# Rotary embedding on VectorE straight out of PSUM, and weight differences kept in DRAM: one change to a four-layer cross-attention kernel

## The reference

```python
vm = expert_mask(token_type_ids)[..., None]
mixed = jnp.where(vm, x @ v_qkv, x @ l_qkv)          # two experts, one per token
q, k, v = jnp.split(mixed, 3, axis=-1)
q, k = apply_rotary(q, k, position_ids, l)           # q * cos + rotate_half(q) * sin
ctx = sdpa(q, k, v, causal=True)
...
v_out = jax.nn.silu(mi @ v_gate) * (mi @ v_up) @ v_down
l_out = jax.nn.silu(mi @ l_gate) * (mi @ l_up) @ l_down
hidden_states = hidden_states + jnp.where(vm, v_out, l_out)
```

## Time and profile before

| | |
|---|---|
| Median of 3 runs | 2689.42 us (2686.3 to 2690.03) |
| The profiled execution | 2684.68 us, span of its instructions 2682.8 us |
| PE busy | 2560.8 us (95%), of it 109.3 us in pauses |
| DVE, ACT, POOL busy | 1534.7 us (57%), 1222.7 us (46%), 1155.9 us (43%) |
| Granted PE clock | 0.993 of full speed, mean over the span |
| DMA | 109.61 MB, 41 GB/s on average |

### The profile page before, as it was taken

One profiled execution on the slowest core, in us unless ns is written; L12 is line 12 of the kernel. 1 busy time (PEld: TensorE's weight loads), 2 busy tenths in 40 slices (PEclk: granted clock), 3 DMA queues, 4 the chain that ended last, 5 costly groups with the idle time before them and its releaser, 6 DMA issues.

```text
span 2682.8 us, 54240 instructions
## 1 busy us (share of the span) xinstructions
PE 2560.8 (95%) x20342; PEld 1554.7 (58%) x20342; DVE 1534.7 (57%) x3448; ACT 1222.7 (46%) x4274; POOL 1155.9 (43%) x1242
## 2 busy tenths in 40 slices
PE   6999999999999999999999999999999999999998
PEld 3556556665565656566555565665656556566565
DVE  2537556766434646776644464677644456467763
ACT  2335444644333635464433362654544346265462
POOL 0025265665211527656410342765641034267564
PEclk9999999999999999999999999999999999999999
DMA  8010011112201011121220101112121000120211
GB/s 211 1 32 2 22 44 48 41 41 72 72 2 32 2 41 40 32 58 31 70 68 1 32 2 52 38 28 60 29 72 60 9 25 2 52 60 10 55 41 44
DMA packets 171100, 109.61 MB, mean 41 GB/s; under 512 B 31764, under 2 KB 168408, under 8 KB 170712
## 3 DMA queue, kind: packets, MB, share of 16 engines
q1 hardware_dynamic: 166384, 105.82, 14.2%
q10 hardware_dynamic: 4456, 0.29, 0.2%
HBM read 101.87 MB, written 4.19 MB: 40 GB/s over the span
## 4 chain that ended last, share of the span: by engine, by line
PE 82%; DVE 11%; POOL 2%; issue 2%; ACT 1%; ACTq 1%; DMA 0%; SPq 0%; DVEq 0%
PE bank L1358 10%; PE bank L1375 6%; PE bank L1081 6%; PE bank L995 5%; PE bank L1244 4%; PE bank L1251 4%; PE bank L1263 4%; PE bank L1272 4%; PE bank L1364 3%; PE bank L1116 2%; PE bank L1298 2%; PE bank L1098 2%; PE bank L1057 2%; PE bank L1224 2%; PE bank L1070 2%
## 5 line engine op out<-in xcount | busy, mean ns | idle before, releaser
L1861 POOL TENSOR_TENSOR Ebuf<-Ebuf,row_rcp 128x512 f32<-128x512 f32 (+1 forms) x328 | 345.8, 1060 | 797.4 <-DVE row_rcp L1684 796.3
L1463 ACT ACTIVATE Ebuf<-bank,minus_max 128x64 f32<-128x64 f32 x1312 | 392.4, 334 | 39.8 <-DVE minus_max L1668 39.5
L1668 DVE TENSOR_REDUCE minus_max<-bank 128x8 f32<-128x512 f32 (+1 forms) x328 | 219.8, 673 | 161.2 <-PE bank L1070 81.2
L1463 ACT ACTIVATION_READ_ACCUMULATOR Ebuf<-bank,minus_max 128x1 f32 x1312 | 297.4, 227 | 0.0
L1472 ACT ACTIVATE PT<-bank 128x512 f32<-128x512 f32 (+1 forms) x328 | 192.6, 601 | 152.5 <-PE bank L1081 151.0
L1081 PE MATMUL bank<-ident,Ebuf 128*128 128x128 f32 x1296 | 201.5, 283 | 9.9 <-POOL Ebuf L1861 9.4
L1081 PEld LDWEIGHTS bank<-ident,Ebuf 128*128 128x128 f32 x1296 | 146.4, 143 | 64.5 <-issue 39.2
L1358 PE MATMUL bank<-xs_a,w_ring 128*128 128x512 f32 (+1 forms) x384 | 172.2, 611 | 7.7 <-POOL w_ring L1909 7.3
L1358 PE MATMUL bank<-xs_b,w_ring 128*128 128x512 f32 (+1 forms) x384 | 169.1, 602 | 5.9 <-POOL w_ring L1909 3.9
L1456 ACT ACTIVATE Ebuf<-Ebuf 128x512 f32<-128x512 f32 x160 | 102.0, 638 | 101.6 <-DVE Ebuf L1673 99.5
L1908 POOL TENSOR_TENSOR w_ring<-w_ring 128x256 f32<-128x256 f32 x192 | 131.9, 708 | 0.0
(11 more groups left out here) (325 smaller groups left out, 5599.6 us busy)
## 6 DMA issues: line engine op xcount, KB each, us to landing
w_ring<-in_L_W SPq DMA_DIRECT2D x64, 256.0 KB, 3.0
w_ring<-in_L_l_gate SPq DMA_DIRECT2D x80, 128.0 KB, 2.2
w_ring<-in_L_l_up SPq DMA_DIRECT2D x80, 128.0 KB, 2.3
w_ring<-in_L_l_down SPq DMA_DIRECT2D x80, 128.0 KB, 2.2
w_ring<-in_L_v_gate SPq DMA_DIRECT2D x80, 128.0 KB, 2.4
w_ring<-in_L_v_up SPq DMA_DIRECT2D x80, 128.0 KB, 2.4
w_ring<-in_L_v_down SPq DMA_DIRECT2D x80, 128.0 KB, 2.5
arena_a<-in_x SPq DMA_DIRECT2D x4, 512.0 KB
```

The costliest lines, as they stand in the source:

```text
L1463: last = A(Ebuf[:, u % UNITS, cell], bank(token)[:, cell], ACT.Exp, bias=minus_max[:, u % UNITS, c:c + 1], accum_out=row_sum[:, u % UNITS, ...
L1668: V.reduce_max(minus_max[:, u % UNITS, 0:g], cells(bank(token)[:, 0:g * S]), AX_X, negate=True).then_inc(maxed, 1)
L1861: G_.tensor_tensor(v, v, row_rcp[:, n % 3, 0:g].unsqueeze(2).broadcast_to([P, g, S]), ALU.mult).then_inc(probs_ready, 1)
```

## The change

Two things are edited, and both change the plan from which every engine's list is made.

**Rotary.** Steps `rot` and `rope` go; `qk` is now planned on PE and DVE. DVE multiplies the bank with the cosines, shuffles the same bank, multiplies with the sines and adds. ACT's copy and POOL's multiply go. The bank is free after the shuffle (`turned`).

**Differences.** Only group 0 (stream a, turn 0) runs `weigh`, and SP writes each difference to a DRAM tensor. All later chunks load expert l (three transfers) and the difference (one transfer, three for the last chunk); `g` waits for these transfers alone.

```diff
-    for i, (step, *where) in enumerate((("qk", 0), ("qk", 1), ("rot", 0), ("qk", 2), ("rot", 1), ("rope", 0), ("qk", 3),
-                                       ("rope", 1), ("rot", 2), ("v", 0), ("rot", 3), ("rope", 2), ("rope", 3), ("v", 1))):
+    for step, *where in (("qk", 0), ("qk", 1), ("qk", 2), ("qk", 3), ("v", 0), ("v", 1)):
...
+def first_use(token):
+
+    return token[1:3] == (0, 0)
...
-    return order
+    return [(when, token) for when, token in order if token[0] != "weigh" or first_use(token)]
...
-    if step == "rot":
-        return [("DVE", 1.45, None), ("POOL", 2.4, None)]
...
-BANK_FREE = {"g": 0.55, "sums": 0.25}
+BANK_FREE = {"g": 0.55, "qk": 1.45, "sums": 0.25}
...
+def begins_chunk(token):
+
+    return token[0] == "g" and not first_use(token) or token[0] == "l1h" and token[3] % 2 == 0
...
+    scratch = nc.dram_tensor("differences", (2 * FT, P, 3, DT * P), F32).ap()
...
-                for e in "lv":
+                if not first_use(key):
+                    q.wait_ge(*kept_at(layer, j))
+                    for dst, src in zip(rarer(rare_share(ring), j), rarer(scratch[FT * (layer - 2) + j], j)):
+                        q.dma_start(dst, src).then_inc(here, 16)
+                for e in "lv" if first_use(key) else "l":
...
+                elif step == "keep":
+                    n, j = where[2:]
+                    ring, _ = chunk("ffn", *where)
+                    q.wait_ge(weighed, FT * (n - 2) + j + 1)
+                    for dst, src in zip(rarer(scratch[FT * (n - 2) + j], j), rarer(rare_share(ring), j)):
+                        q.dma_start(dst, src).then_inc(kept_at(n, j)[0], 16)
...
-                            pe.wait_ge(*weighed[s].at(turn, FT * (n - 2) + j + 1))
+                            pe.wait_ge(*((weighed, FT * (n - 2) + j + 1) if first_use(token) else there))
...
-                if step == "qk":
-                    if where == [3, 0]:
-                        act.wait_ge(*hv_early[s].at(turn, FT))
-                    act.wait_ge(*filled(token))
-                    A(st.qk[:, where[1], :], bank(token)[:, :], ACT.Copy).then_inc(qk_ready[s].sem, 1)
...
-                if step == "rot":
+                if step == "qk":
...
+                    dve.wait_ge(*filled(token))
+                    V.tensor_tensor(by_batch(x), by_batch(bank(token)[:, :]), cos, ALU.mult).then_inc(cosined[s].sem, 1)
...
+                    V.stream_shuffle(v, bank(token)[:, :], PARTNER).then_inc(turned[s].sem, 1)
                     dve.wait_ge(*turned[s].at(turn, k + 1))
...
+                    V.tensor_tensor(by_batch(v), by_batch(v), sin, ALU.mult).then_inc(sined[s].sem, 1)
...
+                    V.tensor_tensor(x, x, v, ALU.add).then_inc(roped[s].sem, 1)
...
-                if step == "rot":
-                    n, i = where
-                    v = by_batch(st.qk[:, i, :])
-                    pool.wait_ge(*turned[s].at(turn, 4 * (n - 2) + i + 1))
-                    G_.tensor_tensor(v, v, cos_sin[:, 0, :].unsqueeze(1).broadcast_to([P, G, S]), ALU.mult).then_inc(cosined[s].sem, 1)
```

More of the change, by code:

```diff
@@ L324, in follows @@
             "zero_s": of("PE", ("wo", JT - 1)), "res2": of(None, ("w2", NF - 1)), "l1h": of(None, ("spread", 2, 0)) + of("PE", ("w2", (last or 0) - 3)),
[L325 to L326 removed]
+            "w2": of(None, ("l1h", last)), "res3": of(None, ("down", n, FT - 1)),
+            "cv": of(None, ("keys", n, 3)), "ck": of(None, ("keys", n, 3)) + of("PE", ("scores", ("self", n, 7))),
             "dense": of(None, ("pv", ("self", n, 4 * (last or 0) + 3))), "cq": of(None, ("spread", 4 if n == 2 else 7, last)),
@@ L396, in inputs @@
             for engine, t, name, *at in follows(step, turn, where):
+                if name == "weigh" and not first_use(token):
+                    continue
                 other = (name, s if name != "table" else 0, t, *at)
@@ L417, in room @@
             return slot()
-        if step == "l1h" and where[0] % 2 == 0:
+        if begins_chunk(token):
             there, free = slot(), banks(1)
@@ L503, in schedule @@
             heads[step, s].pop()
-            if step == "weigh":
-                chunks.append((("ffn", s, turn, *where), ("down", s, turn, *where)))
             if step == "l1h" and where[0] % 2 == 0:
                 chunks.append((("f1", s, turn, where[0] // 2), ("w2", s, turn, where[0] + 1)))
+            elif step == "weigh" or begins_chunk(token):
+                chunks.append((("ffn", s, turn, *where), ("down", s, turn, *where)))
             for j, (other, _, follow) in enumerate(pieces):
@@ L569, in transfers @@
         found.append((END[CHUNK_ENDS[n - SLOTS], "PE"] if n >= SLOTS else -1.0, ("chunk", *chunk)))
+    for token in ORDER["POOL"]:
+        if token[0] == "weigh":
+            found.append((END[token, "POOL"], ("keep", *token[1:])))
     return [token for _, token in sorted(found, key=lambda v: v[0])]
@@ L813, in emptied @@
         if step == "qk":
-            return qk_ready[s].at(turn, 4 * li + last + 1)
+            return turned[s].at(turn, 4 * li + last + 1)
         if step == "v":
@@ L836, in sums, with loads, kept_at, rarer @@
         return [banks[BANK["sum", m, accumulation(token)]] for m in range(DT)]
+    def loads(key):
+        return 2 if key[0] == "f1" else 6 if first_use(key) or key[4] == FT - 1 else 4
+    def kept_at(n, j):
+        m = CHUNKS["ffn", 0, 0, n, j]
+        before = [c for c, k in CHUNKS.items() if c[0] == "ffn" and first_use(c) and k <= m and k % SLOTS == m % SLOTS]
+        return kept[m % SLOTS], sum(16 * (3 if c[4] == FT - 1 else 1) for c in before)
+    def rarer(v, j):
+        if j < FT - 1:
+            return [v]
+        return [v[:, m, :].rearrange("p (k n) -> p k n", k=DT)[:, :, 0:FR] for m in range(2)] + [v[0:FR, 2, :]]
     def chunk(*key):
         n = CHUNKS[key]
-        count = sum(16 * (2 if c[0] == "f1" else 6) for c, m in CHUNKS.items() if m <= n and m % SLOTS == n % SLOTS)
+        count = sum(16 * loads(c) for c, m in CHUNKS.items() if m <= n and m % SLOTS == n % SLOTS)
         return w_ring[:, n % SLOTS, :], (chunk_loaded[n % SLOTS], count)
@@ L925, in load_chunk @@
                         q.wait_ge(*down_done[s].at(turn, FT * (where[0] - 2) + where[1] + 1))
+                    if step == "down" and first_use(CHUNK_ENDS[n - SLOTS]):
+                        q.wait_ge(*kept_at(*where))
                 here = chunk_loaded[n % SLOTS]
@@ L973, in _ @@
                 q.wait_ge(*stored[s].at(TURNS, 0))
+            for n in (2, 3):
+                for j in range(FT):
+                    q.wait_ge(*kept_at(n, j))
         @block.tensor
@@ L1343, in stages @@
                         rows = P if j < FT - 1 else FR
-                        ring, _ = chunk("ffn", s, turn, n, j)
+                        ring, there = chunk("ffn", s, turn, n, j)
                         w = ffn_weights(ring)[0][step]
```

33 lines of the change are left out of this document (16 added, 17 removed), and 2 rows, old and new, of the table own.

## The result

The changed kernel takes 2660.87 us (median) against 2689.73 us on the same chip, 28.9 us less: ratio 0.989, 95% interval 0.987 to 0.9909. One of its four executions was slow, 4284.32 us at a granted clock of 0.554, and is not in the ratio; the median of the other three is 2658.74 us, 31.0 us less than before. Timed again on another chip, the same kernel gave 2660.44 us and 0.9897 (0.9881 to 0.9914). The forecast was 2675 us: the sign was right and the time lies in the range, but the gain was more than double the 14.2 us of the sum.

The account below looks back on a forecast made before the run. PE was taken to bound the kernel, with only pauses and idle time able to change. Terms of -8.4, -11, +3.2 and +2 gave -14.2 us, from 2689.4 to 2675 us, range 2650 to 2695.

Parts of the forecast that it names:

- the sum: Total of the priced terms over the whole kernel: -8.4 - 11 + 3.2 + 2 = -14.2 us.
- What bounds it: PE bounds the kernel, busy 2560.8 of 2682.8 us; only 109.3 us of pauses and 122.0 us idle can change.
- the count of turns: Savings at `g` and the norm chain were counted for three of four turns, with turn 0 gaining nothing.
- 2451.5 us of PE's work, which the change leaves alone: PE's busy time without pauses, taken as unchanged by the edit.
- Norm chain, -11 (0 to -13): `spread`'s waits for DVE's norm links beside POOL's differences: three waits a turn, 1.2 us each, three turns.
- Wait of `g`, -8.4: PE's 11.2 us of waits at `g` for POOL's differences: three quarters go, -8.4 us.
- Transfers, 0: Loads of the kept differences before `g`, and turn 0's 16 writes, stay hidden: 0 us.
- Rotary, 0: Rotary block on DVE, 3.0 us against 2.79; PE waits only 0.2 us for keys, so 0 us.
- New plan, +3.2 and +2: Twelve more pauses on PE cost 3.2 us; pauses moved at stream a's norm 6 cost 2 us (0 to 6).
- The contention goes everywhere: Rival, chance 0.22: POOL's relief halves norm waits (23 us) and cuts waits for probabilities by a third; 2655 us.
- It gives nothing: Rival, chance 0.16: pauses run whether needed or not, so PE waits elsewhere and gives the gain back; 2687 us.
- DVE becomes late: Rival, chance 0.14: the unsplit rotary block delays norm links and maxima on DVE, 0.4 us per block; 2702 us.

Follow-up runs that it names:

- e6: The changed kernel itself, unaltered, timed once more on another chip: 2660.4 us, ratio 0.9897 to the kernel before.
- e1: Kernel before with only the differences made once and kept in DRAM; rotary, order and pauses as before: 2654.0 us, ratio 0.9872.
- e4: e1 with POOL doing subtractions of the same size and number in a spare buffer that nobody waits for: 2678.6 us, ratio 0.9965.
- e5: e4 with POOL's spare subtractions replaced by memsets, which write but read nothing: 2666.1 us, ratio 0.9914.
- e3: Kernel before with both edits, differences and rotary, but the old plan (order and 414 pauses): 2653.7 us, ratio 0.9874.
- e9: e3 with each step's pauses raised by a quarter, 529 for 414: 2652.3 us, ratio 0.9868.
- e10: e4 with the spare subtractions of each chunk done twice: 2771.4 us, ratio 1.0315.
- e2: Kernel before with only the rotary moved to DVE; differences and plan as before: 2681.4 us, ratio 0.9975.

## Why the prediction was right in sign and short in size

**What bounds it** stood in the main: idle time fell by 26.9 us where the sum had 17.4 (8.4 + 11 - 2). The mechanism was the one forecast, and two steps of the sum failed.

**The first step that failed is the count of turns.** "A quarter is turn 0's, where the differences are still made, so 3/4", and again "in the three turns that lose it: 3 x 3 x 1.2". `first_use` is `token[1:3] == (0, 0)`, stream a of turn 0 alone: 12 of that turn's 24 chunks. I had counted 84 of 96 gone for POOL's time and then went by 72 in both terms that matter. This is worth 6 us: 3.3 at the norm chain and 2.6 at `g`, the two waits of turn 0 that the changed kernel doesn't have. Turn 0 has the same stalled chain as the earlier trace rows, in the kernel before:

```profile
502.00 1.41 POOL L1908 TENSOR_TENSOR w_ring<-w_ring 128x256 f32<-128x256 f32 x2
...
502.77 0.65 DVE L1719 TENSOR_TENSOR norm_a<-norm_a 128x2 f32<-128x2 f32 x1
...
505.03 0.40 PE L1217 MATMUL bank<-ident,norm_a 128*128 128x128 f32 x2 [1.52 <-DVE norm_a L1731]
```

**The second is "2451.5 us of PE's work, which the change leaves alone"**, a term put at nothing. That work is not the same from one execution to the next. The changed kernel has 2454.9 us of it in one profiled execution, at a mean granted clock of 0.991, and 2448.3 in the other (e6), at 0.994, with idle times 1.8 us apart. The profiled execution of before had a clock of 0.993. Over its 37 executions beside the experiments those at 0.993 took 2684.7 us on average and those at 0.990 took 2689.9. My two profiled executions stand 9.3 us closer together than the medians, and the clocks fit: the one of before had a high clock for its kernel, the one of the changed kernel a low one (0.991, for 0.992 and 0.993 of its two others). Between before and e6, whose clocks are 0.993 and 0.994, the spans differ by 27.1 us: idle time -25.1, pauses +1.2, own work -3.2.

**Norm chain, -11 (0 to -13).** Setting the 104 `spread` steps of before and e1 side by side, 14 waits became shorter by more than 0.4 us, 16.6 us together: 3.3 in turn 0, 3.8 in each of turns 1 and 2, 5.7 in turn 3. The 3.6 us that I took for a turn was about right; turn 0 and two waits in turn 3, of 0.98 and 1.17 us, were missing. e4 and e5 show the mechanism, contention with POOL's subtractions and not with its memsets. The bound of 13 was too tight for e1; in the changed kernel the new plan gives back 3.6 us and 13.1 are left.

**Wait of `g`, -8.4.** Measured 9.4 in e1 and 11.2 in the changed kernel, where not even turn 0's is left.

**Transfers, 0.** Right: no wait for DMA at `g`, landing 3.5 us, and the 16 writes of turn 0 cost nothing that PE shows.

**Rotary, 0.** Right beside the differences (e3 against e1). By itself it is worth 6.3 us (4.0 to 9.4), and what the trace shows of it is 4.8 us less at `g`, by way of POOL's queue. The prediction didn't see that, since it set the rotary's price by PE's waits for the keys alone.

**New plan, +3.2 and +2.** The sum of 5.2 is near what was measured (4.5, from nothing to 9), but this is luck in part. The second part comes from turn 0 and not from norm 6: after the five pauses of stream a's norm 6 PE waits 0.06 us, not 0.3. The first part is not shown: e9 adds 24.1 us of pauses at no cost.

**The sum again** with these sizes: -11.2 (`g`) - 16.7 (norms) + 3.6 (norms, given back by the new plan) + 1.7 (pauses) - 2.6 (other waits) + 3.4 (own work) = -21.8 us, the difference of the profiled executions. The other 9.3 us are not in these two traces; they go with the clocks, as above. In e9, e1, e4 and e10 PE's own work goes with idle time (2440.1, 2448.5, 2451.3, 2482.7 us for 80.2, 94.8, 115.3, 177.7), as if idle time cost more than itself; that the change won some own work in this way is likely (the seven executions of the changed kernel that the ratios rest on have a mean clock of 0.992, the 37 of before 0.991), but not shown.

**The rivals.** "The contention goes everywhere" has nearly the right time (2655 to 2660 us) for partly wrong reasons: norm waits fell by 13 to 17 us and not 23, and the waits for probabilities didn't fall (9.4 to 10.2). "It gives nothing" and "DVE becomes late" are out: the pauses didn't eat the gain, and no wait for a bank that the shuffle frees, nor more than 0.4 us for L1716 (the old L1668), appears at PE.

## What to carry to other kernels

Price an auxiliary engine's work by what runs beside it: a short dependent chain on DVE, with PE waiting at its end, pays for POOL's subtractions and multiplies beside it, and removing these can be worth more than the wait for their result (here 15 to 17 us of waits against 9 to 11). Count how often an edit bites by its own condition in the code (stream and turn here), not by a round number of turns. Two edits that relieve one queue need not add up (33.7 and 6.3 us alone, 34.1 together); price each with the other in place. When two profiled executions are compared, compare their granted clocks too: 0.003 went with 5 us between executions of one kernel.

## What the runs showed of the hardware

- A DVE TENSOR_TENSOR or SCALAR_TENSOR_TENSOR of two columns took 0.16 us beside POOL's memsets (129 of 129 in e5), 0.57 to 0.65 us beside subtractions of 256 columns (0.71 to 0.78 us each), and 0.96 us beside multiplies of 512 (1.0 us each). The integer TENSOR_SCALAR of the chain took 1.17 us where a memset followed on a multiply beside it, and 0.78 us where a subtraction did.
- The rotary's instructions that read PSUM took 681 to 686 ns (multiply) and 726 to 728 ns (shuffle) in e2, in e3 and in the changed kernel, with POOL busy for 32% to 39% of the span.
- Extra work on POOL that nobody waited for cost 24.6 us for the first 174 us (37% to 43% of the span) and 92.8 us for the next 181 (to 48%).
- In the old plan 529 pauses for 414 cost nothing net: what they took came back as idle time not spent and as PE's own work at a higher granted clock (0.996 for 0.991 to 0.992). In the new plan without any the clock was 0.950 and the kernel 56 us slower than e6.
